# A decoder layer with routed experts on one core: new orders of the steps, centred keys in place of a layer norm, an earlier slot table, and TensorE's expert tiles written out

## What is computed

```python
x = x + attn(layernorm(x))            # (4, 256, 256): gate, value and query projections, a decaying scan over the sequence, output projection
x = x + xattn(layernorm(x), ctx)      # kv = ctx @ W_k.T + b_k
...
    out = jnp.einsum('bij,bjd->bid', p, kv)
    sim = jnp.einsum('bid,bjd->bij', out, kv) * scale
    mu = jnp.mean(sim, axis=-1, keepdims=True)
    var = jnp.var(sim, axis=-1, keepdims=True)
    sim = (sim - mu) * jax.lax.rsqrt(var + EPS) * ln_gamma + ln_beta
    attn = jax.nn.softmax(sim, axis=-1)
...
x = x + ffn(layernorm(x))             # router over 8 experts, one expert for each token, and a shared expert for all
```

## Time and profile before

| | us |
|---|---|
| median of three runs | 152.68 (152.44 to 154.26) |
| the profiled execution | 153.2, span 151.4 |
| busy, share of the span: PE, DVE, ACT, POOL | 77%, 61%, 42%, 58% |

### The profile page before, as it was taken

How to read it: one execution, slowest core, us unless ns; L and a number is a source line. 1 busy time by engine, 2 the same in 40 slices (tenths; PEclk the granted TensorE clock), 3 DMA queues, 4 the chain that set the end, 5 groups by cost and what they waited for, 6 DMA issues and landing times.

```text
span 151.4 us, 2634 instructions
## 1 busy us (share of the span) xinstructions
PE 116.8 (77%) x679; PEld 93.2 (62%) x680; DVE 92.8 (61%) x284; ACT 64.2 (42%) x156; POOL 88.0 (58%) x137
## 2 busy tenths in 40 slices
PE   0299999999886989768989703999999939969700
PEld 0187798977683667556879401788868628748400
DVE  2644498579999999989464470267447246174410
ACT  3346879756778179370811001143144042142100
POOL 5224298946668668748785900256657717737550
PEclk9999999999999999999999995599999999999975
DMA  4997624442231500894044806534332411201000
GB/s 141 215 292 166 233 74 142 135 141 71 74 71 51 157 0 4 266 366 142 0 143 163 285 33 185 175 89 131 88 107 62 160 52 47 87 2 44 28 0 0
DMA packets 18204, 17.48 MB, mean 116 GB/s; under 512 B 4108, under 2 KB 17424, under 8 KB 18192
## 3 DMA queue, kind: packets, MB, share of 16 engines
q1 hardware_dynamic: 15792, 13.56, 30.2%
q0 software_dynamic: 1824, 3.22, 6.7%
q10 hardware_dynamic: 576, 0.56, 1.1%
HBM read 13.78 MB, written 5.38 MB: 127 GB/s over the span
## 4 chain that ended last, share of the span: by engine, by line
PE 49%; DVE 19%; issue 9%; POOL 8%; DMA 5%; another core or an unknown queue 3%; ACT 2%; SPq 1%; POOLq 0%; ACTq 0%; DVEq 0%
PE bG L889 12%; PE bQ L889 10%; PE bV L1096 5%; PE bO L1096 3%; DMA ez<-in_ctx_dram 3%; PE bV L889 3%; POOL x_sorted L427 3%; DVE bn L667 3%; PE bV L1045 3%; PE bO L970 2%; POOL rstd L404 2%; PE bT L1067 2%; DVE res L750 2%; DVE z L738 2%
## 5 line engine op out<-in xcount | busy, mean ns | idle before, releaser
L449 POOL DMA_INDIRECT tq<-base_rows,tid x15 | 15.4, 1027 | 15.9 <-DMA base_rows<-res 10.2
L454 POOL DMA_INDIRECT out_dram<-z,tid x15 | 15.2, 1015 | 13.2 <-DVE z L854 4.8
L434 POOL TENSOR_TENSOR gu_lo<-stage,gu_hi 128x512 fp32r<-128x512 f32 x16 | 20.4, 1289 | 2.2 <-ACT gu_hi L499 2.1
L475 ACT ACTIVATE xn<-res,shift,rstd 128x256 f32<-128x256 f32 x22 | 12.0, 596 | 6.0 <-POOL shift L408 5.8
L427 POOL DMA_INDIRECT x_sorted<-xs,dest x8 | 8.5, 1060 | 5.8 <-DVE dest L781 3.6
L404 POOL TENSOR_TENSOR rstd<-vareps,expo 128x2 f32<-128x2 f32 x16 | 11.6, 725 | 0.4
L400 POOL TENSOR_SCALAR vareps<-mv 128x2 f32<-128x2 f32 x16 | 3.6, 225 | 13.1 <-DVE mv L670 12.4
L667 DVE BATCH_NORM_STATS2 bn<-res 128x6 f32<-128x256 f32 x24 | 8.9, 414 | 3.1 <-DMA res<-in_x_dram 3.1
L840 DVE SCALAR_TENSOR_TENSOR tg<-tg,bG 128x256 f32<-128x256 f32 x8 | 3.4, 420 | 10.8 <-ACT tg L622 8.5
L499 ACT CAST gu_hi<-stage 128x512 fp32r<-128x512 f32 x16 | 9.7, 618 | 0.0
L616 ACT CAST xT_hi<-bT 128x256 fp32r<-128x256 f32 x8 | 3.0, 375 | 15.7 <-PE bT L1067 13.7
(11 more groups left out here) (186 smaller groups left out, 354.5 us busy)
## 6 DMA issues: line engine op xcount, KB each, us to landing
stage<-in_L_ffn_gate_w_dram SPq DMA_DIRECT2D x8, 256.0 KB, 2.7
stage<-in_L_ffn_up_w_dram SPq DMA_DIRECT2D x8, 256.0 KB, 2.7
dn<-in_L_ffn_down_w_dram SPq DMA_DIRECT2D x8, 256.0 KB
xs<-x_sorted SPq DMA_DIRECT2D x15, 136.0 KB
res<-in_x_dram SPq DMA_DIRECT2D x4, 256.0 KB, 3.5
base_rows<-res SPq DMA_DIRECT2D x4, 256.0 KB, 2.7
x_sorted<-pad SPq DMA_DIRECT2D x5, 136.0 KB
x_sorted<-pad ACTq DMA_DIRECT2D x4, 136.0 KB
```

The source lines that it names most:

```text
L434: g.tensor_tensor(units[n][2], stage[:, n % RING], f32(units[n][1]), ALU.subtract).then_inc(unit_lo, 1)
L449: g.indirect_dma_start(rb[:, s % TILE_RING, :], None, base_rows, bass.IndirectOffsetOnAxis(tid[:, s:s + 1], 0), bounds_check=N - 1, oob_is ...
L454: g.indirect_dma_start(out_rows, bass.IndirectOffsetOnAxis(tid[:, s:s + 1], 0), ry[:, s % 2, :], None, bounds_check=N - 1, oob_is_err=Fals ...
L475: last = a.activation(dst[:, i, :], res[:, b * TB + i, :], ACT.Identity, bias=shift[:, kind, b, i:i + 1], scale=rstd[:, kind, b, i:i + 1])
```

## The change

It has five parts. The tables have other orders. norm2 and rstd2 are gone: the keys are centred over the sequence once (`centre_kv`, from sums that kv_bias now makes), so the raw residual can be turned and scored, and the layer norm's scale goes into the epsilon of the similarity's variance (`sim_eps`). The centring of the similarity is gone with it; `sim_scale` scales by the deviation and gamma, then adds beta and takes the minimum of the negated sum in one instruction, and the exponential has scale -1. SyncE stores no base rows before the padding, and all four behind the first row loads. `slot_table` stands behind the last `destination`. PE's fifteen tiles are written out, with one reading of all expert numbers ahead of the first tile.

```diff
 POOL_ORDER = """
-    weight_lo:17 scale_rows:2 scatter:2 scale_rows:3 scatter:3 weight_lo:18 weight_lo:19
+    scatter:1 scatter:2 scale_rows:3 scatter:3 weight_lo:16 weight_lo:17 weight_lo:18 weight_lo:19
     weight_lo:20
...
-            for b in range(B - 2):
-                store_base(b)
...
-            for b in range(B - 2, B):
+            for b in range(B):
                 store_base(b)
...
+            def sim_eps(b):
+                pool.wait_ge(stats[LN2], b + 1)
+                g.tensor_scalar(eps_row[:, b, :], mv[:, LN2, b, :, 1], SIM_EPS / SIM_SCALE ** 2, LN_EPS * SIM_EPS / SIM_SCALE ** 2,
+                                ALU.mult, ALU.add).then_inc(eps_row_made, 1)
...
-            def norm2(b):
-                if b >= 1:
-                    act.wait_ge(sm["t2_done"], b)
-                normalise(LN2, b, xn2, "xn2_made")
...
-                a.activation(kvT_all[:, 2 * h:2 * h + 2, :], (psU, psM)[h][0:C], ACT.Identity,
-                             bias=bk[:, :]).then_inc(kvT_made[h], 1)
+                for i in range(2):
+                    last = a.activation(kvT(2 * h + i), (psU, psM)[h][0:C, i, :], ACT.Identity, bias=bk[:, :],
+                                        accum_out=kv_sum[:, 2 * h + i:2 * h + i + 1])
+                last.then_inc(kvT_made[h], 1)
...
-            def sim_centre(b):
+            def centre_kv(h):
+                dve.wait_ge(kvT_made[h], 1)
+                v.tensor_scalar(kv_mean[:, 2 * h:2 * h + 2], kv_sum[:, 2 * h:2 * h + 2], 1.0 / S, None, ALU.mult).then_inc(kv_mean_made, 1)
+                dve.wait_ge(kv_mean_made, h + 1)
+                for c in (2 * h, 2 * h + 1):
+                    last = v.tensor_scalar(kvT(c), kvT(c), kv_mean[:, c:c + 1], None, ALU.subtract)
+                last.then_inc(kv_centred[h], 1)
+
+            def sim_scale(b):
...
+                for i in range(TB):
+                    last = v.scalar_tensor_tensor(psS[:, i, :], psS[:, i, :], rstd[:, SIM, b, i:i + 1], gam[:, :],
+                                                  ALU.mult, ALU.mult)
+                last.then_inc(sm["scaled"], 1)
+                dve.wait_ge(sm["scaled"], b + 1)
                 if b >= 1:
                     dve.wait_ge(sm["exp_made"], b)
                 for i in range(TB):
-                    last = v.scalar_tensor_tensor(z[:, i, :], psS[:, i, :], rstd[:, SIM, b, i:i + 1], bet[:, :],
-                                                  ALU.mult, ALU.add)
+                    last = v.tensor_tensor_reduce(z[:, i, :], psS[:, i, :], bet[:, :], -1.0, LARGE, ALU.add, ALU.min,
+                                                  nmax[:, b, i:i + 1])
                 last.then_inc(sm["z_made"], 1)
-                dve.wait_ge(sm["z_made"], b + 1)
-                v.tensor_reduce(nmax[:, b, :], z[:, :, :], AX.X, ALU.max, negate=True).then_inc(sm["max_made"], 1)
...
-                pe.wait_ge(sm["xn2_made"], b + 1)
+                pe.wait_ge(sm["x2_made"], (b + 1) * TB)
...
-                turn(psU, xn2, "t2_done")
+                turn(psU, res[:, b * TB:(b + 1) * TB, :], "t2_done")
...
             pe.wait_ge(table_made, 1)
+            e = experts(0, NS)
             pe.wait_ge(unit_lo, len(units) - PROJ)
             pe.wait_ge(small_in["dn"], 16 * E)
...
-            e = experts(0, PEEL + 2)
...
-            for s in range(PEEL):
-                hidden_turn(s, s % 2, s >= 2)
+            for s in range(NS + 1):
+                if s < NS:
+                    hidden_turn(s, s % 2, s >= 2)
...
-            with pe.Fori(0, ROUNDS) as i:
-                e = experts(i * TILE_RING + (PEEL - 1), TILE_RING + 3)
```

More of the change, by code:

```diff
@@ L34 @@
 PE_ORDER = """
[L35 to L41 removed]
+    turn1:0 turn_ctx:0 turn_wk:0 turn_ctx:1 gate:0 value:0 query:0 kv:0 kv:1 turn1:1 recall:0 gate:1
+    turn_kv:0 value:1 turn2:0 query:1 context_mix:0 turn1:2 similarity:0 recall:1 turn1:3 gate:2
+    turn2:1 value:2 query:2 context_mix:1 gate:3 similarity:1 recall:2 query:3 turn2:2 turn3:0
+    value:3 router:0 context_mix:2 similarity:2 router_turn:0 recall:3 shared_gate:0 turn3:1 turn2:3
+    shared_up:0 rank:0 context_mix:3 router:1 similarity:3 shared_up:1 router_turn:1 shared_gate:1
+    turn3:2 shared_down:0 router:2 shared_gate:2 rank:1 router_turn:2 shared_up:2 rank:2 turn3:3
+    shared_down:1 router:3 router_turn:3 rank:3 shared_down:2 shared_gate:3 shared_up:3
     shared_down:3
@@ L56 @@
+    weight_hi:15 router_copy:1 weight_hi:16 score_tanh:1 norm3:2 shared_tanh:1 weight_hi:17
+    turned3_hi:2 softmax_exp:3 router_copy:2 score_tanh:2 norm3:3 turned3_hi:3 shared_tanh:2
+    weight_hi:18 weight_hi:19 router_copy:3 score_tanh:3 shared_tanh:3 weight_hi:20
 """.split()
 DVE_ORDER = """
-    stats1:0 norm1:0 weight_lo:0 weight_lo:1 turned1_lo:0 stats1:1 stats1:2 weight_lo:2 turned1_lo:1
-    stats1:3 memory:0 turned1_lo:2 residual2:0 memory:1 residual2:1 memory:2 sim_stats:0
-    sim_centre:0 turned1_lo:3 sim_scale:0 residual2:2 sim_stats:1 sim_centre:1 residual3:0
@@ L62 @@
-    sim_scale:1 memory:3 residual3:1 turned3_lo:0 residual2:3 sim_stats:2 route:0 sim_centre:2
-    destination:0 sim_scale:2 turned3_lo:1 shared_hidden:0 residual3:2 sim_stats:3 route:1
-    sim_centre:3 sim_scale:3 destination:1 turned3_lo:2 residual3:3 shared_hidden:1 route:2
-    destination:2 turned3_lo:3 shared_hidden:2 shared_add:0 route:3 destination:3 shared_add:1
-    shared_hidden:3 shared_add:2 shared_add:3 slot_table:3
+    stats1:0 norm1:0 weight_lo:0 turned1_lo:0 weight_lo:1 weight_lo:2 stats1:1 stats1:2 memory:0
@@ new lines @@
+    centre_kv:0 turned1_lo:1 centre_kv:1 residual2:0 stats1:3 memory:1 turned1_lo:2 sim_stats:0
+    residual2:1 sim_scale:0 turned1_lo:3 memory:2 residual3:0 sim_stats:1 residual2:2 sim_scale:1
+    turned3_lo:0 memory:3 residual3:1 sim_stats:2 route:0 residual2:3 sim_scale:2 turned3_lo:1
+    shared_hidden:0 residual3:2 sim_stats:3 route:1 destination:0 sim_scale:3 turned3_lo:2
+    shared_hidden:1 residual3:3 route:2 destination:1 shared_add:0 destination:2 turned3_lo:3
+    shared_hidden:2 shared_add:1 route:3 destination:3 slot_table:3 shared_add:2 shared_hidden:3
@@ L67 @@
+    shared_add:3
 """.split()
 POOL_ORDER = """
-    rstd1:0 rstd1:1 rstd1:2 weight_lo:3 rstd1:3 weight_lo:4 weight_lo:5 weight_lo:6 weight_lo:7
-    rstd2:0 weight_lo:8 weight_lo:9 rstd2:1 weight_lo:10 sim_rstd:0 weight_lo:11 weight_lo:12
-    rstd2:2 sim_rstd:1 rstd3:0 weight_lo:13 weight_lo:14 weight_lo:15 rstd3:1 rstd2:3 sim_rstd:2
-    scale_rows:0 weight_lo:16 scatter:0 rstd3:2 sim_rstd:3 scale_rows:1 scatter:1 rstd3:3
-    weight_lo:17 scale_rows:2 scatter:2 scale_rows:3 scatter:3 weight_lo:18 weight_lo:19
+    rstd1:0 rstd1:1 rstd1:2 weight_lo:3 sim_eps:0 rstd1:3 weight_lo:4 weight_lo:5 sim_rstd:0
@@ L75 @@
+    weight_lo:6 weight_lo:7 weight_lo:8 sim_eps:1 rstd3:0 sim_rstd:1 weight_lo:9 weight_lo:10
+    weight_lo:11 weight_lo:12 sim_eps:2 rstd3:1 sim_rstd:2 weight_lo:13 weight_lo:14 sim_eps:3
+    scale_rows:0 rstd3:2 sim_rstd:3 scale_rows:1 weight_lo:15 scatter:0 rstd3:3 scale_rows:2
+    scatter:1 scatter:2 scale_rows:3 scatter:3 weight_lo:16 weight_lo:17 weight_lo:18 weight_lo:19
     weight_lo:20
@@ L593, in shared_tanh @@
                 a.activation(hs[:, b % 2], psG, ACT.Tanh, scale=0.5).then_inc(sm["th_made"], 1)
-            steps = {"norm1": norm1, "norm2": norm2, "norm3": norm3, "weight_hi": weight_hi, "turned_wk": turned_wk, "turned_ctx": turned_ctx, "kv_bias": kv_bias,
+            steps = {"norm1": norm1, "norm3": norm3, "weight_hi": weight_hi, "turned_wk": turned_wk, "turned_ctx": turned_ctx, "kv_bias": kv_bias,
                      "turned_kv": turned_kv, "mixed": mixed, "turned1_hi": turned1_hi, "gate_tanh": gate_tanh,
```

80 lines of the change are left out of this document (28 added, 52 removed).

## The result

The changed kernel takes 156.95 us in the median of four runs (156.58 to 157.41), the kernel before beside it 153.31 us (152.44 to 154.26): 1.024 times the time, with an interval of 1.016 to 1.032. It is slower, by 3.6 us, and the interval leaves out 1; whether by more than 2% it leaves open. The prediction said 151.0 us, range 147 to 156.

The account below looks back on a forecast made before the run. PE and VectorE were taken to share the bound up to 80 us, then the seam and PE's back-to-back tiles. 153.2 - 2.9 + 5.0 - 4.0 = 151.3, stated as 151.0 us since the profile stands 0.5 over the median; range 147.0 to 156.0.

Parts of the forecast that it names:

- Part 1: Front, up to the last scatter: norm2 removal and new orders end scatter:3 at 80.3 us, not 83.16: -2.9 us.
- The fused minimum: Front, VectorE: fused add-and-minimum with a read of the accumulator, taken at 0.55 us each, between 0.44 and twice that.
- the walk through the orders: Front: both orders followed with old durations; residual2:0 starts at 21.3 us and residual3:3 ends at 67.7 instead of 69.76.
- Rival (b): Front, VectorE: the fused minimum costs double, 0.42 us more each, 3.4 us at the last scatter: 154.7 us; chance 0.14.
- Part 2: Seam, last scatter to first row transposition: SyncE's queue waits behind unit 20, 15.1 us against 10.1: +5.0 us.
- splitting and wake-up: Seam: weight_lo:16 on GpSimd behind scatter:3, with its wake-up, takes 1.35 us before SyncE can load unit 20.
- unit 20 and the down weights: Seam: SyncE's load of weight unit 20 and eight dn loads, queued behind weight_lo:16, take 5.31 us.
- landing of the last: Seam: the fourth region's padding lands 2.3 us after its issue, as the row loads take.
- the early table: Seam: slot table made at 79 to 80 us instead of 90.4, worth nothing behind SyncE's queue with unit 20.
- Part 3: PE's tile stage: written-out tiles remove the loop's gaps and the late signals seen in it: -4.0 us, other end -1.6.
- Rival (a): Tile stage: late signals belong to ACT's and VectorE's loops or the chip; part 3 gives 1.6 us: 153.7 us; chance 0.25.

Follow-up runs that it names:

- combined: Changed kernel with weight_lo:16 ahead of scatter:0, down weights loaded ahead of unit 20, and GpSimd waiting for the slot table before weight_lo:17: 147.0 us, no ratio.
- after_w16_early: Changed kernel with GpSimd's splitting weight_lo:16 moved back ahead of scatter:0: 150.16 us, 0.979 times the kernel before.
- after_dn_first: Changed kernel with SyncE's eight loads of the down weights issued ahead of the load of unit 20: 149.55 us, 0.977 times the kernel before.
- no_gather: after_dn_first without GpSimd's fifteen gathers of base rows, so the base is left out of the output: 140.29 us; with TensorE's loop put back, 142.12 us.
- before_pe_flat: Kernel before with only TensorE's tiles written out and all fifteen expert numbers read ahead of the first tile: 154.65 us, 1.012 times the kernel before.
- after_pe_loop: Changed kernel with TensorE's tile loop of the kernel before put back: 157.65 us, 1.026 times the kernel before.
- table_first: after_dn_first with GpSimd waiting for the slot table ahead of weight_lo:16: 150.38 us, 0.980 times the kernel before.

## Why the prediction was wrong

**Part 1, -2.9 us: right in mechanism, too small.** It brought 4.4 us. VectorE ended residual3:3 3.8 us earlier, not 2.1. The fused minimum cost 0.77 us for two where 1.1 was taken, and residual2:0 started at 19.7 us where the walk through the orders gave 21.3. Centring the keys cost 0.3 us each as said, with 0.16 us for the mean that was not counted. Rival (b), the double price, is out.

**Part 2, +5.0 us: right, 1.2 us too small.** The first transposition came at 95.06 us, forecast 95.4, but from an earlier scatter. Term by term: splitting and wake-up 1.4 (1.35), unit 20 and the down weights 4.7 (5.3), padding and counts 1.2 (1.8), four paddings 2.2 (1.8), landing of the last 4.4 (2.3), row loads 2.2 (2.3). The mis-sized term is the landing: the price was that of row loads on an idle queue, and here 2 MB of down weights were ahead. They are not the whole of it, as in combined, without them, the landing took 3.8 us. after_w16_early and after_dn_first show that the queue was the cause, since either takes some 6 us out of the seam. The sentence that the early table is worth nothing behind this queue holds; with the queue mended combined's seam is 4.0 us shorter than that of the kernel before. Not foreseen was VectorE's 5.6 us beside GpSimd: the table was made at 83.8 us and not at 79 to 80. In the changed kernel it stayed hidden; it was the next bound as soon as the queue was mended.

**Part 3, -4.0 us: wrong, and this is the step that failed.** It read: "They stand between the loop's start and its end and nowhere else, so I take it that they go with it." That the late signals stood inside the loop was where they were seen, not why. They stand in the tiles, and the loop covers most of them; so do GpSimd's gathers and writes, which the earlier trace rows do not show. The changed kernel has no loop and the same idle time of PE in the stage, 13.3 against 13.6 us. Putting the loop back changed nothing, and taking away the gathers or the indirect writes took the late signals away but for one bout. Rival (a) placed them in the other loops, or in the chip, which was nearer; but it still gave the loop 1.6 us, of which 1.31 were a late signal too, and no_gather with and without the loop shows no gap at it. The 2.5 us that the stage got longer were in no case of the prediction. They are PE's busy time at half clock behind two stalls inside the tiles. The prediction weighed the clock at the seam, and not inside the stage. Against the forecast of 54 us, 4.0 us of the miss are the stalls that stayed and 2.5 the clock behind them.

**The sum.** Measured by stretches: -4.4 + 6.2 + 2.5 = +4.3 us of span, and 3.6 in the medians. Forecast: -2.9 + 5.0 - 4.0. The front and the seam alone would have given 153.2 + 1.8 = 155.0 us, within the range; the rest is part 3.

**What stays open.** How two indirect transfers a tile delay PE's signals is not shown, only that the bouts go when one of the two is taken away. Their spacing points at something besides the transfers themselves: tiles and transfers come every 2.7 us, the bouts in several kernels every 10 us. Nor is it shown that they come in an execution whose trace is not taken. Whether writing out PE's tiles makes falls of the clock likelier is open too: before_pe_flat is 2.0 us slower than its base, after_pe_loop no faster than its own, and written-out kernels had both kinds of stage.

## What to carry to other kernels

A wait that is seen only inside some construct is not yet caused by it: list what else runs there and nowhere else, above all on engines that the wait does not name, and take the nearest suspect away before its cost is booked as a gain. When work is moved later on one engine, follow the load that waits for it, and then everything that stands behind that load in its queue; the first thing to mend is the order, which here was worth 7 us of 157 for one word. A stall costs twice where the clock falls behind it, so a forecast for a stage with stalls needs a term for busy time as well as one for idle time.

## What the runs showed of the hardware

- PE's signals can be late by up to 4 us while PE's products are recorded as done. In after_w16_early, for work that ended at 107.04 and 107.26 us, VectorE and ACT started at 110.63 and 110.67; bouts ended at 100.7, 110.7, 120.8 and 130.9 us there, in table_first at 100.8, 110.7, 121.1 and 131.1, and in after_pe_loop at 107.1, 117.2, 127.4 and 137.3. Signals of ACT and VectorE were on time in the same stretches: PE started at 109.07 us on a result that VectorE finished at 109.01. The front, with its scatters and weight loads, had no wait without a known releaser in any run.
- With fifteen indirect gathers and fifteen indirect writes of GpSimd in the stage it took 57 to 60.7 us in nine kernels, with one kind left 49.4 to 53.3 us where no queue of SyncE's stood in the way.
- A VectorE operation on one partition and fifteen numbers took 5.6 us in all eight kernels in which GpSimd's splitting of 128x512 weights ran beside it, and 0.15 us in the six in which it did not.
- A stage with the same 210 to 211 matmul instructions had PE busy for 41.0 us at a mean clock of 0.98 and for 47.7 us at 0.84.
- In the changed kernel PE's waits of 2.1 and 1.8 us inside the tiles were each followed by some 3.4 us at half clock; in the kernel before one of 2.4 us was not.
